# First layer: one matmul of 259 columns for high weights by high and low values, and sums in two sets of four banks

## The reference

```
h = relu(layernorm(x))
# layer 0 (the first)
wh  = h @ W;  wh1 = wh @ a[:128];  wh2 = wh @ a[128:]
e   = leaky_relu(wh1 + wh2.T, 0.2);  e = where(adj > 0, e, -9e15)
x   = x + elu(softmax(e) @ wh)
# layer 1 (the second)
h   = relu(layernorm(x))
Qn, Kn = cos_normalize(h @ Wq.T), cos_normalize(h @ Wk.T)
att = softmax(where(adj > 0, Kn @ Qn.T, -9e15))
x   = x + 0.5 * (att @ h, or h for a row without neighbours) + 0.5 * h
```

## Time and profile before

| what | value |
|---|---|
| median of 3 runs | 2208.91 us (2207.93 to 2211.29) |
| the profiled execution: its own time, its span | 2208.86 us, 2207.1 us |
| mean granted TensorE clock | 0.994 |
| PE, weight load (PEld), DVE, ACT busy | 2156.9 (98%), 1748.4 (79%), 1986.9 (90%), 1642.4 us (74%) |
| first layer's main part | 52 to 773 us of the span |
| DMA in it, moved | 0.99 to 1.02 busy, 374 to 402 GB/s (from 110 to 700 us) |
| DMA in layer 1 | 0.59 busy, 204 GB/s (from 900 us on) |

### The profile page before, as it was taken

How to read it: one execution, slowest core, us unless ns; L and a number is a source line. 1 busy time by engine, 2 the same in 40 slices (tenths; PEclk the granted TensorE clock), 3 DMA queues, 4 the chain that set the end, 5 groups by cost and what they waited for, 6 DMA issues and landing times.

```text
span 2207.1 us, 62831 instructions
## 1 busy us (share of the span) xinstructions
PE 2156.9 (98%) x26133; PEld 1748.4 (79%) x26133; DVE 1986.9 (90%) x1717; ACT 1642.4 (74%) x1446; POOL 1.4 (0%) x9
## 2 busy tenths in 40 slices
PE   5999999999999979999999999999999999999998
PEld 5999999999999966777777777777777777777776
DVE  7999999999999889898898888888898888988887
ACT  5777778877788667777777777777777777777776
POOL 0000000000000000000000000000000000000000
PEclk9999999999999999999999999999999999999999
DMA  6899999999999924565655665665656556665653
GB/s 253 309 365 398 390 403 399 399 402 396 399 401 388 374 72 148 200 215 194 221 206 206 208 216 199 211 212 198 222 197 212 212 196 220 208 207 206 219 195 114
DMA packets 153482, 573.23 MB, mean 260 GB/s; under 512 B 9888, under 2 KB 10336, under 8 KB 152928
## 3 DMA queue, kind: packets, MB, share of 16 engines
q1 hardware_dynamic: 144096, 549.78, 68.2%
q10 hardware_dynamic: 9216, 20.98, 2.4%
HBM read 558.11 MB, written 12.62 MB: 259 GB/s over the span
## 4 chain that ended last, share of the span: by engine, by line
PE 88%; DVE 7%; issue 4%; ACT 1%; DMA 0%; DVEq 0%; POOL 0%; ACTq 0%; POOLq 0%
PE bank L1068 30%; PE bank L1002 27%; PE bank L1089 21%; PE bank L1084 10%; DVE ring L791 4%; DVE hl_buf L816 1%; DVE hl_buf L717 0%; DVE norm L805 0%; DVE v_buf L823 0%; DVE q_buf L823 0%; PE bank L1029 0%; ACT hl_buf L422 0%; ACT ring L538 0%; DMA r_ring<-a_rows 0%; DVE stats L752 0%
## 5 line engine op out<-in xcount | busy, mean ns | idle before, releaser
L538 ACT ACTIVATE ring<-bank 128x1024 f32<-128x1024 f32 x512 | 524.1, 1024 | 348.2 <-PE bank L1068 346.0
L849 DVE SCALAR_TENSOR_TENSOR ring<-ring 128x2048 f32<-128x2048 int32 x256 | 586.5, 2291 | 158.7 <-ACT ring L538 158.7
L1002 PE MATMUL bank<-v_buf,ring 128*128 128x129 f16 (+1 forms) x12288 | 713.4, 220 | 7.2 <-DVE ring L791 6.4
L1002 PEld LDWEIGHTS bank<-v_buf,ring 128*128 128x128 f16 x12288 | 708.5, 98 | 12.1 <-issue 11.1
L1068 PE MATMUL bank<-v_buf,q_buf 128*128 128x512 f16 x3072 | 704.8, 379 | 2.3 <-ACT ring L538 1.3
L1089 PE MATMUL bank<-u_buf,hl_buf 128*128 (+1 forms) x8192 | 704.3, 220 | 0.0
L1089 PEld LDWEIGHTS bank<-u_buf,hl_buf 128*128 128x128 f16 x8192 | 631.9, 98 | 55.8
L791 DVE SCALAR_TENSOR_TENSOR ring<-r_ring,th_word,ring 128x1024 f32<-128x1024 f32 x512 | 619.8, 1277 | 24.7 <-ACT ring L474 22.0
L854 DVE TENSOR_TENSOR hl_buf<-ring,hl_buf 128x2048 f16<-128x2048 f32 x256 | 584.5, 2284 | 0.0
L1084 PE MATMUL bank<-u_buf,hl_buf 128*128 (+1 forms) x2048 | 557.9, 272 | 0.2 <-DVE hl_buf L854 0.2
L474 ACT ACTIVATE ring<-ring 128x2048 f32<-128x2048 int32 x256 | 481.0, 1908 | 93.6 <-DMA ring<-adj 89.8
(11 more groups left out here) (105 smaller groups left out, 445.9 us busy)
## 6 DMA issues: line engine op xcount, KB each, us to landing
ring<-adj SPq DMA_DIRECT2D x512, 1024.0 KB, 5.5
r_ring<-a_rows SPq DMA_DIRECT2D x8, 512.0 KB, 7.1
x_dram<-q_buf ACTq DMA_DIRECT2D x8, 512.0 KB, 7.4
h_dram<-hl_buf ACTq DMA_DIRECT2D x8, 512.0 KB, 7.2
hl_buf<-h_dram SPq DMA_DIRECT2D x16, 256.0 KB, 2.7
r_ring<-x_dram ACTq DMA_DIRECT2D x16, 256.0 KB, 3.8
r_ring<-h_dram ACTq DMA_DIRECT2D x16, 256.0 KB, 4.1
out<-r_ring ACTq DMA_DIRECT2D x16, 256.0 KB, 4.4
```

Of the source, the lines that this page charges most:

```text
L538: nc.scalar.activation(p_ring[:, k, hf * 1024:(hf + 1) * 1024], bank[:, 2 * hf:2 * hf + 2, :].rearrange("p b n -> p (b n)"), ACT.Exp, scal ...
L849: V.scalar_tensor_tensor(p_ring[:, k, :], adj_ring[:, k, :], 0.0, p_ring[:, k, :], ALU.is_gt, ALU.mult).then_inc(s_m, 1)
L1002: ins = mm(acc0(par, it), weights0(k, ps)[:, it // 4, jj, f], v2[:, bass.ds((2 * j + us) * VW, D + 1)], start=False, stop=False, skip_grou ...
```

## The change

For the even blocks of a chunk the products high by high and high by low become one matmul. The high and the low values of one tile lie side by side in `v_buf` (130 fp16 columns apart), so a moving operand of 259 columns takes both; its result is 259 columns wide, the high sums in columns 0 to 128 and the low sums in 130 to 258. The low weights still multiply the high values in a matmul of 129 columns, added to the high sums. Odd blocks keep their three matmuls of 129. A step has 40 matmuls in place of 48, and 6200 moving columns in place of 6192.

A pair of blocks now takes 388 columns of a bank, so a set of eight sums takes four banks: even chunks 0 to 3, odd ones 4 to 7. The transposes and projections between the layers move to other banks (`ht_bank` 2 and 3, `qk_banks` 0, 1 and 4, 5, `qkt_bank` 6 and 7).

In the epilogue the low sums have to be added. After step 3 VectorE copies the odd denominators and the low denominators, adds the low to the high ones, and takes one reciprocal of eight: four small instructions, two of which wait for the one ahead. After step 7, ahead of the negative part, it adds the four blocks of low sums, each times its reciprocal, to the quotients (four instructions of 128 columns), and the negative part waits for them. The preset can come only once the low sums have been read, so it moves from step 5 to step 9, behind the exponential; it is three instructions of 520, 516 and 516 columns in place of 387, 387 and 258. Between the layers `qk(1, 1)` waits for that adding in place of the quotients.

```diff
@@ sums and banks
+WIDE = VW + D + 1
-EPI0 = ("den", "neg", "elu", "x1", "stats") + LN + ("hi", "lo")
+EPI0 = ("densum", "den", "low", "neg", "elu", "x1", "stats") + LN + ("hi", "lo")
         def acc0(par, it):
-            b, k = 3 * par + it // 3, it % 3
-            return bank[:, b, k * (D + 1):(k + 1) * (D + 1)]
+            k = it % 2
+            return bank[:, 4 * par + it // 2, k * WIDE:k * WIDE + D + 1]
+        def acc0_wide(par, it):
+            return bank[:, 4 * par + it // 2, 0:WIDE]
+        def acc0_column(par, col):
+            return bank[:, 4 * par:4 * par + 4, col]
         def ht_bank(r):
-            return bank[:, 6 + r, :]
+            return bank[:, 2 + r, :]
         def qk_banks(r):
-            return bank[:, 2 * r:2 * r + 2, :].rearrange("p b n -> p (b n)")
+            return bank[:, 4 * r:4 * r + 2, :].rearrange("p b n -> p (b n)")
         def qkt_bank(i):
-            return bank[:, 4 + i, :]
+            return bank[:, 6 + i, :]
@@ ScalarE
             def preset(par):
-                for i in range(3):
-                    g = acc0_group(par, i)
-                    ins = nc.scalar.activation(g, v_sum[:, :].unsqueeze(1).to_broadcast([P, g.shape[1], D + 1]),
+                sums = bank[:, 4 * par:4 * par + 4, 0:WIDE + D + 1]
+                nc.scalar.activation(sums[:, :, D + 1:WIDE].rearrange("p b (s n) -> p b s n", s=2),
+                                     ident[:, 0:D // 2 + 1].unsqueeze(1).unsqueeze(1).to_broadcast([P, 4, 2, D // 2 + 1]),
+                                     ACT.Copy, scale=0.0)
+                for k in range(2):
+                    ins = nc.scalar.activation(sums[:, :, k * WIDE:k * WIDE + D + 1],
+                                               v_sum[:, :].unsqueeze(1).to_broadcast([P, 4, D + 1]),
                                                ACT.Copy, scale=EMPTY)
                 ins.then_inc(s_pre, 1)
...
                     ins.then_inc(s_free, 1)
-                    if not (isinstance(c, int) and c == NC0 - 1):
-                        act.wait_ge(s_free, c + 1)
-                        act.nop(nofuse=True)
-                        preset(par)
                 def exponential():
                     act.wait_ge(s_ev, at("neg"))
                     nc.scalar.activation(e_buf, e_buf, ACT.Exp).then_inc(s_ea, 1)
+                    if c != NC0 - 1:
+                        preset(par)
@@ VectorE
                 def denominators():
                     dve.wait_ge(s_used, U0 * (c + 1))
-                    for b in range(3):
-                        g = acc0_group(par, b)
-                        ins = V.reciprocal(den[:, 0, 3 * b:3 * b + g.shape[1]], g[:, :, D])
-                    ins.then_inc(s_ev, 1)
+                    V.tensor_copy(den[:, 1, 1:IT0:2], acc0_column(par, WIDE + D))
+                    V.tensor_copy(den[:, 2, 0:IT0:2], acc0_column(par, VW + D)).then_inc(s_ev, 1)
+                    dve.wait_ge(s_ev, at("densum"))
+                    V.tensor_tensor(den[:, 1, 0:IT0:2], acc0_column(par, D), den[:, 2, 0:IT0:2], ALU.add).then_inc(s_ds, 1)
+                    dve.wait_ge(s_ds, c + 1)
+                    V.reciprocal(den[:, 0, :], den[:, 1, :]).then_inc(s_ev, 1)
                 def negative():
                     dve.wait_ge(s_free, c + 1)
+                    for it in range(0, IT0, 2):
+                        f = slice(it * P, (it + 1) * P)
+                        ins = V.scalar_tensor_tensor(z_buf[:, f], acc0_wide(par, it)[:, VW:VW + D], den[:, 0, it:it + 1],
+                                                     z_buf[:, f], ALU.mult, ALU.add)
+                    ins.then_inc(s_ev, 1)
+                    dve.wait_ge(s_ev, at("low"))
                     V.tensor_scalar(e_buf, z_buf, 0.0, None, ALU.min).then_inc(s_ev, 1)
@@ TensorE
-                                for ps, us in parts:
+                                if it % 2 == 0:
+                                    mm(acc0_wide(par, it), weights0(k, 0)[:, it // 4, jj, f],
+                                       v2[:, bass.ds(2 * j * VW, WIDE)], start=False, stop=False, skip_group_check=True)
+                                for ps, us in parts[2:] if it % 2 == 0 else parts:
...
             qk(0, 0, True)
             t2(2, 0)
-            pe.wait_ge(s_free, NC0)
+            pe.wait_ge(s_ev, len(EPI0) * (NC0 - 1) + EPI0.index("low") + 1)
             qk(1, 1, True)
```

6 lines of the change are left out of this document (2 added, 4 removed).

## The result

The changed kernel takes 2216.64 us, the median of 6 runs (2213.02 to 2219.96), against 2209.39 us (2207.56 to 2211.29) for the kernel before on the same chip: a ratio of 1.0035 with a 95% interval of 1.0025 to 1.0045. So it is slower, by 7.2 us, where 2210.2 us were forecast and 2203 to 2215 us were the range. Timed again, beside its variants, it took 2214.68 us (ratio 1.0030, 1.0018 to 1.0042), a median inside the range; but each of the twelve executions, 2211.72 us the shortest, lies over the 2210.2 us that were forecast. In the table of experiments one much longer execution each of e2 (2246.59 us) and e7 (2358.89 us), both at a lower granted clock, is outside the ratios, and without it the median of e2 is 2212.05 us.

The account below looks back on a forecast made before the run. The prediction took layer 0 as bound by DMA (88.2 us a chunk) and TensorE (88.1) together, VectorE near; start +0.05, layer 0 -0.3, between layers +1.6 made +1.35 on 2208.86: 2210.2 us, range 2203 to 2215.

Parts of the forecast that it names:

- 0.044 us less a step: Layer 0 matmuls on TensorE: 40 in place of 48 take 2.71 us a step, bounds 0 and 0.06 saved.
- Rival D: Layer 0 steps: the wide matmul saves nothing, a step stays at 2.75 us; 2212.1 us, chance 0.09.
- VectorE's work: Epilogue: low sums 1.17 us with their wait, denominators +0.4, together 1.55 us a chunk; covered in chunk 6.
- rival C: Epilogue: small instructions cost full length, gates of chunks 1 to 7 move by 2.1 to 3 us; 2213.6 us, chance 0.17.
- the start: Ahead of the first Sign: ScalarE's preset grows by 0.4 us, but VectorE waits there for another DMA; +0.05 us.
- The moved preset: ScalarE, step 5 to step 9: 1.6 us behind the exponential, bounds 1.3 and 2.1, delaying the Sign of step 10.
- That gate moves by +1.6: Step 20 of chunk 6, where TensorE stood on VectorE's pair at 650.67 us, comes 1.6 us later.
- the sum: Whole kernel: start +0.05, layer 0 -0.3, between the layers +1.6, together +1.35 us, giving 2210.2 us.
- 88.2 us a chunk: Layer 0 adjacency supply: the DMA needs about 88.2 us a chunk, beside TensorE's 88.1, so landings can't come sooner.
- Rival A: Layer 0 loads: the DMA has room and VectorE limits next, 87.0 us a chunk; 2205.9 us, chance 0.20.
- Between the layers: VectorE's denominators (+0.4 us) and low sums (1.17 us) have no cover there and delay the serial stretch; +1.6 us.
- The signs that I named: Trace checks: 2.71 us steps, some 10 us of TensorE waits, four-chunk Signs 352 to 354 us apart, layer 0's end within 1 us.

Follow-up runs that it names:

- e2: Kernel before the change, with only its preset moved from behind the quotients at step 5 to behind the exponential at step 9: 2212.41 us, ratio 1.0018.
- e7: Changed kernel, each first-layer adjacency load from the ninth on fetching only one of its two output blocks: 2204.30 us, ratio 0.9979.
- e8: Changed kernel without VectorE's added work (low sums never added to quotients or denominators): 2211.72 us, ratio 1.0013.
- the second trace: Changed kernel profiled once more, unedited, when timed again beside its variants: 2214.68 us, ratio 1.0030.
- e1: Changed kernel with the preset moved from behind the exponential at step 9 to behind the Sign of step 24, last chunk's preset left out: 2207.35 us.
- f3: Changed kernel, preset and row factors' load moved to step 24, ScalarE signalling after each half of the quotients so low sums start earlier: 2205.42 us, ratio 0.9984.
- e5: Changed kernel with preset behind the Sign of step 24 and row factors' load ahead of the loads of step 24: 2206.64 us, ratio 0.9992.
- e4: Changed kernel with the row factors' load issued ahead of the loads of step 24 instead of step 8: 2210.22 us, ratio 1.0008.
- e6: Kernel before the change, with preset behind the Sign of step 24 and row factors' load ahead of step 24's loads: 2207.41 us, ratio 0.9993.
- f1: Changed kernel, step 9's adjacency load of every chunk fetching one of two output blocks, part of SyncE's loop written out: 2209.74 us, ratio 1.0005.

## Why the prediction was wrong

**TensorE: right.** 0.044 us less a step were forecast and 0.04 measured. Rival D (nothing saved) falls.

**VectorE's work: right in size.** 1.12 us for the low sums, copies and sums 0.08 to 0.2 us from start to start; so rival C's full-length instructions fall too. In the inner chunks it is covered (e8), at the first gate it isn't: I counted 0.05 us for the start and nothing for chunks 0 and 1, where the forecast itself said that VectorE sets the pace. That gate came 0.90 us later (1.30 in the second trace).

**The moved preset: right in size and place, wrong in how often it is paid.** This is the step that failed: "That gate moves by +1.6", after which the sum took the gate once, let TensorE gain "32 x 0.044 = 1.4" to the next one, and kept the supply where it was, "because the landings can't come sooner". They can come later. A later step 20 frees the next chunk's slots later, the load is issued later and lands later. The loads of steps 8 to 10 in chunk 6 on SyncE's timeline, before and after:

```profile
598.02 5.86 SPq L263 DMA_DIRECT2D ring<-adj  x3
```

```profile
600.46 5.79 SPq L267 DMA_DIRECT2D ring<-adj  x3
```

The supply was not an independent clock of 88.2 us that the engines read off; it was the last member of a loop. Going round it, the preset adds 1.54 us to the leg of every chunk, and TensorE's faster steps give back only those that lie in the loop, 14 x 0.04 = 0.6, not 32. A part of the rest was taken up by the queue: the loads are asked for later, and step 9's latency fell from 8.1 us in the mean of chunks 2 to 6 to 7.8 and, in the second trace, 7.6. That leaves +0.4 and +0.2 us in each of the first five periods (88.87 and 88.67 us for 88.43), where the sum had TensorE gain 1.4. In the sixth, with no load of row factors ahead of step 9, its latency is 5.4 us and the chunk takes 87.04, TensorE's own. So step 20 of chunk 7 comes 1.97 us later than before, and 1.37 in the second trace, where 0.2 were forecast. Rival C had the right form, a shift that accumulates "from the point where the gate's shift exceeds the 1.4 us that PE gains in a chunk"; my own 1.6 exceeded that already, and by the loop the point was 0.6. One of its signs came too, "a gate more than 3 us later": 3.13 us in chunk 6 (2.52 in the second trace). Its reason, full-length instructions, did not.

**The DMA: the limit was set too high.** I read 88.2 us a chunk as the DMA's need, because it stood there in four chunks and a load was always queued. The rows gave only a part of that a source: 32 landings are 81.6 us and three half-megabyte transfers at the same pace 3.8, 85.4 together. With the preset out, the same bytes take 87.65 us (e1) and 87.44 (f3), and single chunks 87.1. Rival A (room in the DMA) was half right: there was room for about 0.6 to 0.8 us, which the preset's place took away. No version that moves every byte came to TensorE's own 87.07 us in the mean; e7, with half the bytes, did. What holds the others at 87.4 to 87.7, the loads or VectorE's work as in e5, wasn't found. (A's own sum says 4.6 where its terms, 6 less 1.6, give 4.4.)

The Trainium skill ("DMA: Bandwidth & Descriptors", section Where 436 GB/s comes from) gives 435 GB/s as a ceiling, by which the adjacency of a chunk would be through in 77 us (an estimate from that figure), and has a lower figure, about 358, as what binds between HBM and SBUF. The trace lies between the two: with loads queued, ScalarE's Signs behind the landings are 2.57 us apart (593.45 and 596.02 in the changed kernel), 408 GB/s.

**Between the layers: right.** +1.6 forecast; 1.5 in the work itself (`qk(1, 1)` starts 4.34 us behind the last matmul of layer 0 for 2.83), 1.7 in the means over kernels. The first pair of traces shows 2.6; the 1.1 beyond the work lies within the spread of traces with the same code.

**The signs that I named.** Right: the step, PE's waits of about 10 us (8.3 in the inner part, 16.1 in all), gates at steps 20 and 12, the size of the low sums. Wrong: the last matmul of layer 0 within 1 us of its old place (1.55 later; 0.93 in the second trace). For four chunks I had named 352 to 354 us between Signs of the same step. The pair of the earlier trace rows, step 4 of chunks 3 and 7, is 353.73 us apart now (330.82 and 684.54), which fits. But it takes in the short last period; from the issue of step 9 in chunk 2 to that in chunk 6 it is 355.30 us, for 353.22 before. The sign was chosen too far down to see the shift.

The Trainium skill ("Perfetto Trace Analysis", section Identifying the Most-Contended Engine) says to optimise the engine with the highest occupancy first, and not to judge TensorE by its matmuls' busy share, but by its weight loads', for one. Over the whole kernel VectorE (90%) then stands ahead of TensorE's weight loads (79%) and of ScalarE (74%). This case goes against the order: without its added work on VectorE the changed kernel takes 3 to 5 us less (e8), while moving 1.6 us of ScalarE's work out of one place gave 7 to 9 us.

**What stays open.** The changed kernel's runs spread over 9 us (2211.72 to 2220.42), and e4's, which also has the preset in the loop, over 8; those of e1, e5 and e6, which don't, over 2 to 3, but f3's, which doesn't either, over 5. The profiled executions of the changed kernel are among its fastest, so the traces show 4 us of a loss of 6 to 7. The rest, which alone carries the median of the first six beyond the range, is in no trace: that it comes from the same loop follows only from the medians of e1 and e2. In the slow chunks that I have (89.7 us in the changed kernel, 91.1 in f1) step 9's load takes 8.7 us, which fits a loop that passes every late landing on to the next chunk; what makes a landing late wasn't tried.

## What to carry to other kernels

Where a ring of buffers is refilled when its last user is done, follow the chain once round: landing, each engine's work, the release of the slot, the issue, the queue, the landing. Work put into that loop is paid in each period, and a faster engine gives back only the steps that lie in the loop; look for a place for the work outside it before anything else. A transfer's constant period is no proof that the transfer sets it: take a microsecond of an engine out of the loop and see whether the period follows.

## What the runs showed of the hardware

The latency of a load from issue to landing is elastic: its median from 200 to 740 us was 3.9 us with half loads, 7.6 and 7.2 in the two traces of the changed kernel, 8.0 in the one before, 8.2 with the late preset (e1) and 8.5 with both moves (e5), so it was longer where the chunks were shorter (88.57, 88.40, 88.39, 87.65 and 87.62 us). Taking a transfer out of the way of step 9's load or halving it (e4, f1) brought its landing 0.2 to 0.7 us a chunk nearer to its issue, where 1.2 or more were expected. And VectorE's four additions with PSUM sources ran at full speed beside ScalarE's reads of other banks: 0.61 us for two in f3, 0.60 in the earlier trace rows.
